# One written order per engine for both layers of a transformer and state-space block

## The reference, cut to what is computed

```python
# 8 batches of 256 tokens, 128 wide; all in fp32
xn = layernorm(x)
q = xn @ Wq + bq; k = xn @ Wk + bk; v = xn @ Wv + bv      # 16 heads, 4 key/value heads of 8
attn = softmax(q k^T / sqrt(8)); a = (attn v) @ Wo + bo
logits = xn @ Wg                                         # 8 experts, the best two kept
f = (g1 + g2) * (relu(xn @ w1) @ w2)                       # all experts share w1 and w2
x = x + a + f
xn = layernorm(x)
xs, z = split(xn @ W_in)                                   # 256 channels each
xs = silu(conv4(xs) + conv_b)
dt = softplus(xs @ W_dt + b_dt); Bs = xs @ W_x             # 16 states
h[s] = h[s] * exp(-A[s] * dt) + Bs[s]                      # a scan over 256 tokens
y = (sum_s h[s] + D * xs) * silu(z); m = y @ W_out
u = silu(xn @ w1' * s1) * (xn @ w2' * s2)                  # 512 wide
u = gelu(u @ h1' * t1); u = gelu(u @ h2' * t2)
x = x + m + (u @ w3') * s3
```

## Time and profile before

| what | value |
|---|---|
| time of three executions | 552.67, 555.87, 557.18 us |
| median | 555.87 us |
| span of the profiled execution | 541.5 us |
| median less span | 14.4 us |
| instructions | 6429 |
| PE busy | 443.2 us (82%) |
| DVE busy | 379.9 us (70%) |
| ACT busy | 296.3 us (55%) |
| POOL busy | 164.5 us (30%) |

### The profile page before, as it was taken

One profiled execution on the slowest core, in us unless ns is written; L12 is line 12 of the kernel. 1 busy time (PEld: TensorE's weight loads), 2 busy tenths in 40 slices (PEclk: granted clock), 3 DMA queues, 4 the chain that ended last, 5 costly groups with the idle time before them and its releaser, 6 DMA issues.

```text
span 541.5 us, 6429 instructions
## 1 busy us (share of the span) xinstructions
PE 443.2 (82%) x1736; PEld 205.7 (38%) x1736; DVE 379.9 (70%) x621; ACT 296.3 (55%) x495; POOL 164.5 (30%) x193
## 2 busy tenths in 40 slices
PE   2589999999999999897767787977879777795886
PEld 1346444445354434222322232622326323362334
DVE  3663527573755747345679996799967999869992
ACT  2112445564646545656888716886247963478411
POOL 2533013213131311301005670055710457205551
PEclk9985569998999989688999998999979999899799
DMA  5716761515233240000000000000000000000000
GB/s 143 109 36 106 236 116 38 92 38 84 45 76 66 46 74 2 2 1 1 0 0 0 1 1 0 1 22 0 0 0 0 19 0 0 0 2 20 0 0 21
DMA packets 36861, 18.94 MB, mean 35 GB/s; under 512 B 5988, under 2 KB 35300, under 8 KB 36836
## 3 DMA queue, kind: packets, MB, share of 16 engines
q1 hardware_dynamic: 36272, 18.56, 16.9%
q10 hardware_dynamic: 564, 0.08, 0.2%
HBM read 13.46 MB, written 4.98 MB: 34 GB/s over the span
## 4 chain that ended last, share of the span: by engine, by line
PE 44%; issue 21%; DVE 19%; ACT 12%; DMA 1%; DVEq 1%; SPq 1%; ACTq 0%
DVE acc L1078 7%; PE bank L247 7%; PE bank L361 6%; PE bank L233 4%; ACT da L968 4%; PE bank L271 4%; PE bank L281 4%; DVE hb L1066 4%; PE bank L784 3%; PE bank L785 3%; DVE mx L483 3%; PE bank L789 2%; PE bank L256 2%; ACT pt L446 2%; PE bank L799 2%
## 5 line engine op out<-in xcount | busy, mean ns | idle before, releaser
L1066 DVE TENSOR_TENSOR_SCAN hb<-da,bank 128x512 f32<-128x512 f32 x128 | 149.1, 1209 | 10.0 <-ACT da L968 10.0
L1141 POOL TENSOR_TENSOR acc<-acc,hb 128x512 f32<-128x512 f32 x60 | 94.3, 1572 | 171.5 <-DVE hb L1066 171.4
L483 DVE TENSOR_REDUCE mx<-bank 128x2 f32<-128x512 f32 x128 | 83.5, 684 | 32.4 <-PE bank L233 31.7
L446 ACT ACTIVATE pt<-bank 128x512 f32<-128x512 f32 x128 | 72.1, 595 | 53.8 <-PE bank L361 52.8
L968 ACT ACTIVATE da<-dt,nega 128x510 f32<-128x510 f32 x128 | 81.8, 710 | 16.0 <-DVE hb L1066 15.8
L799 PE MATMUL bank<-sil,ld_fh 128*128 128x512 f32 x128 | 63.0, 615 | 0.0
L770 PE MATMUL bank<-b_parts,sel 96*128 96x512 bf16 (+1 forms) x64 | 24.6, 394 | 42.3 <-DVE hb L1066 39.8
L233 PE MATMUL bank<-k_sc,q_sc 48*128 48x256 bf16 x256 | 51.6, 300 | 8.2 <-DVE mx L483 8.2
L799 PE MATMUL bank<-gelu,ld_fh 128*128 128x512 f32 x128 | 57.6, 592 | 0.0
L361 PE MATMUL bank<-q_st,k_st 51*128 51x512 bf16 x128 | 50.4, 421 | 2.3 <-ACT pt L446 1.5
L247 PE MATMUL bank<-pt,v_sb 128*32 128x512 f32 x256 | 41.0, 722 | 1.0 <-ACT pt L446 1.0
(11 more groups left out here) (133 smaller groups left out, 619.0 us busy)
## 6 DMA issues: line engine op xcount, KB each, us to landing
q_sc<-q_scr SPq DMA_DIRECT2D x8, 384.0 KB, 4.9
q_st<-q_scr SPq DMA_DIRECT2D x8, 384.0 KB, 5.2
ld_fh<-in_h_t SPq DMA_DIRECT2D x2, 1024.0 KB, 8.3
q_scr<-qk_parts SPq DMA_DIRECT2D x8, 192.0 KB, 2.1
q_scr<-qk_parts SPq DMA_DIRECT2D x8, 128.0 KB, 1.8
out<-x SPq DMA_DIRECT2D x4, 256.0 KB, 2.3
x_sb<-in_x SPq DMA_DIRECT2D x3, 256.0 KB, 5.5
k_sc<-k_scr SPq DMA_DIRECT2D x8, 96.0 KB, 5.3
```

The costliest lines, as they stand in the source:

```text
L446: eng.activation(pt[:, n % 8, :], st_bank[n % 2][:, :], ACT.Exp, scale=HD ** -0.5).then_inc(p_ok, 1)
L483: eng.tensor_reduce(mx[:, 2 * pair:2 * pair + 2, q], s_bank[n % 2][:, :].rearrange("p (h k) -> p h k", h=2), AX.X, ALU.max).then_inc(mx_ok, 1)
L1066: eng.tensor_tensor_scan(hb[:, n % NR, :], da[:, n % NRD, :, :].rearrange("p b n -> p (b n)"), b_bank[s % 2][:, :], 0.0, ALU.mult, ALU.add ...
L1141: TT(acc[:, 1, :], acc[:, 1, :], hb[:, (CI * s + 1) % NR, :], ALU.add).then_inc(acc1, 1)
```

## The change

Loops are gone. Each engine gets one list for the whole program, `ORDERS`, in which `3*S` means three pieces S; pieces of both layers stand in the same list, and each knows its batch or group by counting. So layer 1's first group stands among the last batches of layer 0, and the input part of group `g+1` among the scans of group `g`.

In layer 0: inputs come as a few packed arrays, each loaded by one DMA, and x and the output are laid out by partition. The first eight score tiles of batch 0 are not made from bf16 parts that return from DRAM but from fp32 queries times fp32 keys, copied once for each head and multiplied with a column of 0 and 1 (`own_keys`). The separate copies `q_sc`, `k_sc` are gone: rows 0 to 47 of `q_st` and `k_st` serve the maxima and rows 64 and up the attention. 44 pieces `warm` of two bf16 matmuls each, on constant data, stand before and between the first pieces. All four `pv` groups add up in one bank, so that one copy and four transposes a batch (`o_out`, `heads`) stand where two and eight did. Value and gate weights are one matmul. `normalised` moves from DVE to ACT as an activation with bias minus mean over deviation.

In layer 1: all 128 additions to `acc` are on POOL, and so are the products with D (`start`), with the gate (`y`) and the whole split of B (`split`). Softplus is one activation. silu of z is tanh and one DVE product (`zm`) in all groups, silu of x and of the feed-forward part in group 0. `normalise` is on ACT, with the bias minus mean over deviation computed by POOL (`shifted`). There are 31 decay tiles in place of 16.

Left out of the diff are the packing of the inputs, waits that were only rewritten, and the functions whose body is as before.

```diff
+ORDERS = dict(
+    sync="""x_in head constants0 2*x_in ffn_weights 3*put fetch stack 3*put fetch 2*put 3*rows loads put fetch stack
+        2*put loads 3*rows put fetch stack loads put 3*rows 2*put stack fetch 3*rows stack 3*put fetch 3*rows
+        loads 3*put stack fetch 3*rows stack 3*put fetch 3*rows stack 3*rows 8*out landed""",
+    tensor="""9*warm xn_transposes warm project 2*warm v_gate 8*warm S ffn_in 2*warm xn_transposes S ffn_in 2*S project
+        2*S warm 2*S 2*warm xn_transposes 2*S ffn_out 2*S warm project 2*warm 2*S ffn_in 2*S warm ffn_in
+        xn_transposes max_rows 2*S 4*warm v_gate warm 2*S warm ffn_out A S A S 4*warm A S A S project A S A S
+        4*warm S A S warm ffn_in S A S pv A S A S ffn_in A S A S max_rows ffn_out S A S pv A S v_gate A S A S pv
+        A S A S pv 2*A 2*S heads A S A S pv xn_transposes back A S A S project S A S A proj_out ffn_in max_rows
+        pv A S A S ffn_in A S A S pv A S A S ffn_out A S A S pv A S A S v_gate heads A S A pv A S A back
+        xn_transposes A S A S pv A S A S proj_out project max_rows ffn_in A S A S pv A S A ffn_in A S A S pv A S
+        v_gate ffn_out A S A S heads A S A pv 2*A S back xn_transposes A S pv A S A S ffn_in A S A S proj_out
+        ffn_in max_rows A S project S A S 2*pv S A S A v_gate heads S A S A ffn_out A S A xn_transposes back A S
+        A S pv A S A S project proj_out A S A S pv S A S A pv A S A S max_rows ffn_in pv 2*S ffn_in 2*S heads
+        v_gate S 2*A S ffn_out S A S A back A S A S pv 2*A S proj_out A 2*S A pv A S A ffn_in max_rows 2*A 2*S
+        v_gate ffn_in A S A S pv S A S A pv A S A S ffn_out heads A S A pv A S A S back x_transposes A S A pv A
+        S A proj_out S A S A x_in A S A pv max_rows x_in ffn x_in pv A x_in A ffn A wx A ffn 2*step_in A heads b
+        x_transposes ffn A pv A b x_in A x_in A second b second A x_in b A pv back A second b A second x_in b A
+        wx A proj_out b pv A step_in 2*b pv step_in heads b second back b second b 2*second b proj_out third b
+        2*third b third b third x_transposes third b third b third x_in b ffn b x_in ffn x_in b 2*ffn x_in wx
+        2*second b out b step_in b out second b 4*out x_transposes b 2*second 2*b 2*second x_in second 2*b
+        step_in 2*third b third b x_in b 2*third b 2*third b third x_in b ffn b ffn b x_in ffn 2*out ffn 2*b wx
+        2*second b 3*out b second b 2*second b 2*second b out b second 2*step_in 2*b 2*third b third b 2*third
+        2*b 3*third ffn b ffn b out ffn b ffn b 2*out b out 3*second b 2*second b 2*second b second b 2*out
+        third b 2*third b third b 4*third 6*out""",
+    scalar="""roots deviation0 normalised xn_out deviation0 wide_out own_keys qk_out own_keys normalised own_keys relu
+        xn_out deviation0 gate_exp relu normalised own_keys qk_out xn_out qk_out relu normalised relu
+        negated_maxima gate_exp xn_out 7*E qk_out E relu 2*E relu E negated_maxima E normalised 6*E o_out E
+        gate_exp E decay_rates 2*E xn_out 2*E qk_out 2*E relu negated_maxima 2*E relu 2*E normalised 4*E o_out
+        2*E gate_exp 5*E xn_out 3*E normalised negated_maxima relu 4*E relu E qk_out E o_out 4*E gate_exp 6*E
+        relu 2*E xn_out negated_maxima relu 2*E qk_out o_out 4*E normalised gate_exp 3*E xn_out 9*E
+        negated_maxima relu qk_out o_out relu deviation 2*E gate_exp 10*E negated_maxima relu 2*E relu 4*E o_out
+        gate_exp 2*E normalise 6*E x_out 4*E taps E negated_maxima taps gate_x E sil gate_z gate_x 2*E gate_z
+        sil E o_out E b_in normalise sil 2*dt D E D sil E x_out D E 2*D E D taps 3*D E D taps D E 2*D E 2*D
+        gate_z E 2*gate_x E 2*D E gate_z 2*D E b_in D E 3*D gelu o_out gelu 2*dt 5*D 2*gelu 4*D deviation hid
+        normalise hid D x_out 4*D 2*hid taps 2*D 2*sil taps normalise gate_z sil 2*gate_x sil D gate_z D b_in
+        9*D dt 11*D x_out 2*D gelu taps 3*gelu D dt 8*D taps D hid D 3*hid gate_z gate_x 2*sil gate_x gate_z 4*D
+        2*sil 6*D b_in 9*D 2*gelu 3*D 2*gelu 2*dt 12*D 2*hid D 2*hid 2*sil 4*D 2*sil 10*D 2*gelu 4*D 2*gelu
+        2*hid D 2*hid""",
+    vector="""ones moments inverse moments clear inverse moments first_split v_out 4*M gate_sum 6*M gate_norm 2*M gated
+        2*M inverse 4*M v_out 4*M gate_sum 2*M gate_norm 2*M gated 15*M v_out 2*M heads gate_sum 2*M gate_norm
+        2*M back_out gated M residual 10*M v_out M heads M gate_sum M back_out gate_norm 2*M gated M residual
+        6*M v_out 3*M heads M gate_sum M gate_norm M gated 2*M back_out 2*M residual 5*M v_out 2*M heads M
+        gate_sum back_out 2*M gate_norm 2*M gated 4*M residual 2*M statistics 5*M v_out heads 3*M gate_sum
+        back_out M gate_norm 3*M gated 2*M residual 4*M inverse1 2*M v_out 2*M heads M gate_sum 3*M gate_norm
+        back_out M residual 3*M gated 2*conv clear mul zm 2*xm zm 2*mul scan mul heads scan conv 2*scan conv
+        scan zm back_out scan zm scan residual 2*scan heads clear 2*scan back_out scan residual scan statistics
+        scan inverse1 4*scan conv scan 2*mul conv zm 2*mul scan zm 5*scan residual1 scan residual1 2*scan conv
+        6*scan conv 2*scan zm 2*mul zm 2*scan 2*mul 6*scan 2*residual1 9*scan 2*mul 2*scan 2*mul 6*scan
+        2*residual1 3*scan 2*residual1""",
+    gpsimd="""ones biased 2*G biased 4*G qk_split 2*G qk_split maxima_split 8*G biased qk_split maxima_split 8*G
+        maxima_split qk_split constants 8*G maxima_split G qk_split 7*G maxima_split qk_split 8*G maxima_split
+        qk_split 8*G maxima_split shifted 8*G maxima_split 2*start split 9*add start 3*add start 2*add split
+        14*add shifted 4*add 2*y 18*add start add split 2*add start 11*add 2*y 8*add 2*start 14*add split 11*add
+        y 4*add y 26*add y add y""",
+)
...
+def run_order(order, pieces):
+    count = {name: 0 for name in pieces}
+    for token in order.split():
+        times, _, name = token.rpartition("*")
+        for _ in range(int(times or 1)):
+            pieces[name](count[name])
             count[name] += 1
-        else:
-            pieces[name]()
...
+NPAIR = 4
+ND0, ND1, ND2 = 6, 17, 8
+NRD = ND0 + ND1 + ND2
+TANH_Z, TANH_X, TANH_FFN = (0, 1, 2, 3), (0,), (0,)
...
+        def fetch(b):
+            q_out, k_out = scratch(b)
+            reached(eng, scr_ok, b, 16 * NSTK, 16 * NSTK)
+            reached(eng, s_ps, b - 2, NH, NH)
+            if b < 2:
+                eng.wait_ge(init_p, 2)
+            def k_rows(lo, hi):
+                return eng.dma_start(k_st[b % 2][0:ROWS, lo:hi, :],
+                                     k_out[lo * HD:hi * HD].rearrange("(h d) c n -> (d c) h n", d=HD))
+            def q_rows(lo, hi):
+                return eng.dma_start(q_st[b % 2][0:ROWS, lo:hi, :],
+                                     q_out[lo * HD:hi * HD].rearrange("(h d) c n -> (d c) h n", d=HD))
+            if b == 0:
+                k_rows(NKV // 2, NKV).then_inc(sc0_ok, 16)
+            else:
+                k_rows(0, NKV).then_inc(sc_ok, 16)
+                q_rows(0, NH // 2).then_inc(sc_ok, 16)
+            q_rows(NH // 2, NH).then_inc(sc2_ok, 16)
...
+        def rows(n):
+            b, p = n // NPART, n % NPART
+            reached(eng, *((negm_ok, b, 1, 1) if p == 0 else (msplit, b, 3, (1, 3)[p - 1])))
+            reached(eng, st_ps, b - 2, NH, NH)
+            eng.dma_start(q_st[b % 2][HALF + ROWS + p:HALF + ROWS + p + 1, :, :].rearrange("o h n -> o (h n)"),
+                          m_parts[:, p, :]).then_inc(mrow_ok, 16)
...
         def scores(n):
+            b, n = n // NH, n % NH
+            pair, q = n // TPB, n % TPB
+            if b == 0 and n < NH // 2:
+                eng.wait_ge(own_ok, pair + 1)
+                reached(eng, mx_ok, b, NH, n - 1)
+                mm(s_bank[n % 2][:, :], q_all[:, q * P:(q + 1) * P],
+                   k_own[:, pair, :, :].rearrange("p e n -> p (e n)"), start=True, stop=True).then_inc(s_ps, 1)
                 return
             if n == 0:
+                reached(eng, sc_ok, b - 1, 32, 32)
+            if b == 0 and n == NH // 2:
+                eng.wait_ge(sc0_ok, 16)
+            if n == NH // 2:
+                reached(eng, sc2_ok, b, 16, 16)
+            reached(eng, mx_ok, b, NH, n - 1)
             for j in range(2):
                 last = mm(s_bank[n % 2][:, j * T:(j + 1) * T],
+                          q_st[b % 2][0:ROWS, 2 * pair + j, q * P:(q + 1) * P],
+                          k_st[b % 2][0:ROWS, 2 * pair // G, :],
                           start=True, stop=True)
             last.then_inc(s_ps, 1)
...
+        def pv(n):
+            b, grp = n // 4, n % 4
+            gp, kt = grp // 2, grp % 2
             reached(eng, p_ok, b, NH, 4 * grp + 4)
+            if n == 0:
+                eng.wait_ge(warm_end, 1)
             if grp == 0:
+                reached(eng, o_ok, b, 1, 0)
                 reached(eng, v_ok, b, 1, 1)
+            at = VS * (1 - gp)
             for kv in range(NKV):
```

(84 more changed lines are left out.)

1597 lines of the change are left out of this document (729 added, 868 removed).

## The result

| what | after |
|---|---|
| time of four executions | 382.81 to 383.38 us, median 383.04 |
| before beside it, four executions | 552.67 to 566.2 us, median 556.52 |
| ratio | 0.692, 95% interval 0.688 to 0.697 |
| span of the profiled execution | 381.6 us (its own time 383.38) |

The kernel is 173 us faster. The forecast was 425 with a range of 402 to 458, so it was 42 us too high, and the range didn't hold the time; even the rival in which PE is almost full stood at 404. Direction and bound were right, the size wasn't.

A forecast was written before the change was run, and what follows sets the result against it. PE's work was taken as the bound: 346.7 us at a fill of 0.93 is 372.8; with the first A at 35 and 3 behind PE, 410.8 of span, plus 14.4 gives 425.2 us. Range 402 to 458.

The forecast's parts named there:

- the rival in which PE is almost full: Whole program: PE at a fill of 0.98 and the first A at 33, time 404; chance 0.12.
- first A: Start: first attention matmul at 35 us, between 32 and 50, against 56.2 before; worth 21 us.
- first A to first `b`: Mostly layer 0: 140.2 us of PE work, 151 us at a fill of 0.93.
- first `b` to the end of PE: Layer 1: PE work of 49.3, 49.7 and 48.4 us to each next group's first `b`, then 59.1 to the end.
- behind PE: End: last addition of 0.7 us and the output's DMA of 2.3, taken as 3.
- time less span: Outside the span: the median of before is 14.4 us above its span, added to 410.8 to give 425.2.
- 32 S and A at 0.225 = 7.2: PE in layer 0: price of the S and A matmuls in a batch, 7.2 of 18.7 us.
- the fill of 0.93: PE's 346.7 us of work divided by 0.93 gives 372.8; PE at 0.90 to 0.96 had chance 0.52.
- The old fill of 0.84: Rival: handovers keep before's layer 0 fill as tables change a dozen times a group; time 468; chance 0.20.
- ACT as the bound: Rival in layer 1: a table change holds ACT 1.28 us more, groups of 61 to 65, time 464; chance 0.05.
- GpSimd isn't the bound: Rival judged: additions stay at 1.55 us, so POOL has 58 a group in layer 1, time 441; chance 0.08.
- PE stays at its lower level: Rival: slower than before once 156 us of PE's 347 run at 1.2 GHz; 716 if all did; chance 0.02.

The follow-up runs named there:

- a_same_half: Kernel after with the row halves of S and A swapped in odd batches, so neighbouring S and A share a half in 74 of 98 pairs; 395.61 us.
- a_again: Kernel after, unchanged, measured once more on another chip; 384.23 us.
- a_by_group: Kernel after with layer 1's pieces sorted by group, the input part of group g+1 behind all scans of g; 450.2 us.
- a_one_table: Kernel after with gelu and silu as tanh and softplus as absolute value, so 44 of 50 table loads go; 383.23 us.
- a_scores_dram: Kernel after with batch 0's first eight score tiles made from bf16 parts that come back from DRAM, not fp32 keys; 395.6 us.
- a_layers_apart: Kernel after with all five lists sorted, layer 0's pieces first and layer 1's behind, order inside each layer kept; 427.63 us.

## Why the prediction missed the size

| step | forecast | measured | difference |
|---|---|---|---|
| first A | 35 | 35.65 | +0.7 |
| first A to first `b` | 151 | 127.0 | -24.0 |
| first `b` to the end of PE | 221.8 | 216.0 | -5.8 |
| behind PE | 3 | 2.9 | -0.1 |
| time less span | 14.4 | 1.8 | -12.6 |
| sum | 425.2 | 383.4 (profiled execution) | -41.8 |

**The price of S and A.** The step that failed first is "32 S and A at 0.225 = 7.2". It priced them one behind the other, as the rows of before show them, and didn't look at the rows of PE that their operands stand in. The diff leaves S in rows 0 to 47 and moves A from rows 0 to 50 to rows 64 to 114, and there a pair costs what one cost. By a_same_half this is 0.17 a pair, 17 us for 98 pairs; by full overlap it would be 22 (98 x 0.22 = 21.6, so that 140.2 us of work become 118.6). A batch takes 16.5 us (first five, from first A to first A: 35.65 to 118.05) in place of 20 to 21. At the fill of 0.93, full overlap gives 127.5 us for the stretch and explains all of the 24; 0.17 a pair explains 18 of them, and the other 6 are then a fill of 0.97. The Trainium skill (TensorEngine Tiling (Array Packing), Key Properties) says that each tile of the array is tied to its partitions and that different tiles can execute matmuls in parallel; this case's traces agree, with 0.01 us between the starts of A and S. Read against the diff, full overlap would have put the sum at 402, the low end of the range.

**The outside of the span.** "The median of before is 14.4 above its span; with it, 425.2" added a difference that doesn't belong to the program. In every execution whose own span is known, time less span is 1.7 to 2.1 us (383.38 and 381.6; of before 562.55 and 560.8, 555.16 and 553.4). The profiled execution of before, 541.5, was a short one: the spans of its 32 executions beside the experiments run from 542.0 to 582.7. So the difference was one between two executions. The clock has a part in this spread: the granted clock of these executions lies between 0.86 and 0.932, and the longest have the lowest (0.865 at 582.7, 0.918 at 542.0), but it doesn't explain each of them (0.916 at 547.8, 0.915 at 562.0), and what else there is stays open. A kernel whose clock stays up spreads less: after over 0.6 us (2.4 in a_again), before over 13.5 beside it.

With these two terms right the sum is 35 + 118.6 / 0.93 + 221.8 + 3 + 1.8 = 389, and the 6 us that are left of the miss are the fill of layer 1.

**The fill of 0.93.** Over the first stretch it holds, if pairs overlap in full (118.6 / 127.0 = 0.93); in layer 1 it is 206.5 / 216.0 = 0.956, with the four groups' prices as the 206.5. The old fill of 0.84, which had a chance of 0.20, came about in neither. The groups are 55.7, 50.4, 48.4 and 61.5 against prices of 49.3, 49.7, 48.4 and 59.1: full but for the first and the last. Of the first group's 6.4 too many, 1.8 is the minus mean on POOL. That step stands in the change and was not priced at all; it queues behind additions, as the forecast had described for SP's queue only.

**What held.** PE is the bound, as forecast, and the first A stands where it was put, at the upper level but for the first `warm` (18 matmuls in 3.66 us, later 16 in 1.92). That a serial head is dear is borne out by a_by_group, though its head is a longer one than that of before. Table loads are 1.28 with no gap, 50 of them (53 forecast); a_one_table shows that they cost nothing, or 2 us at the most, so ACT as the bound, by either price of a switch, is refuted. GpSimd isn't the bound, though its additions were mis-sized: 1.268 long and 1.23 apart (13 in 15.94 from 197.93), against 1.15 and 1.12. It is busy for 188 us of 216. The start with fp32 keys was judged rightly as a way around two trips: a_scores_dram prices it at 11 to 13 us. "PE stays at its lower level" didn't come about. Two runs show that PE does fall to it: in a_scores_dram after one pause of 9.2 us, and in a_layers_apart without a long one, after PE had been busy for 2.38 and then 1.47 us of 4 (144 to 152).

**What stays open.** How much of the 173 us is the clock alone: neither run on before settled it. And the parts can't be added up, since both runs that undo an order also let the clock fall. What DVE's relief is worth without the new lists is not shown either.

## What to carry to other kernels

When a change moves matmul operands to other partitions, look at which neighbours in the list then use different rows of PE: a pair of short contractions can cost what one does, no row of the trace before will show it, and it pays where PE is the bound. An order that keeps PE fed pays twice, since a pause also costs the clock behind it; price a wait with the dearer work that follows. Add to a span only what the runs' own spans show beside their times, and look for small instructions on a queue full of long ones.
